# An attention and feed-forward kernel: the load of the next keys asked for by GpSimd behind its seventh subtraction, in place of SyncE ahead of its turns of x rows and forms

## The reference

```python
x = x + xattn(layernorm(x), ctx)       # Q = xn Wq' + bq, K = ctx Wk' + bk
                                       # softmax(Q K' / 32) ctx
x = x + ffn(layernorm(x))              # silu(x Wg') * (x Wu'), then Wd'; weights are
                                       # 4-bit codes, one factor for each block of 64
```

## Time and profile before

| | |
|---|---|
| median of three runs | 1919.1 us |
| the profiled execution | 1918.35 us, its span 1916.2 us |
| granted TensorE clock, mean | 0.999 of full speed |
| busy: PE, DVE, ACT, POOL | 1898.2, 1623.0, 1448.2, 370.3 us |
| GpSimd's subtractions (line 1583) | 64, 893 ns mean |
| transfers of `ctx` by SyncE, 1024 KB each | 8, of which 7 at line 1534 |

### The profile page before, as it was taken

The page is one execution under the profiler, slowest core; times in us unless marked ns, Lnnn a source line. Parts: engine busy times, 40 slices in busy tenths (PEclk is TensorE's granted clock), DMA queues, the critical chain, the costliest instruction groups (busy, mean ns, idle before and its releaser), DMA issues.

```text
span 1916.2 us, 29499 instructions
## 1 busy us (share of the span) xinstructions
PE 1898.2 (99%) x9758; PEld 963.7 (50%) x9758; DVE 1623.0 (85%) x2694; ACT 1448.2 (76%) x2697; POOL 370.3 (19%) x568
## 2 busy tenths in 40 slices
PE   9999999999999999999999999999999999999999
PEld 4487888744444444444444444444444444444444
DVE  7978999869889899899898888898798898896963
ACT  3887776588998988988988988988999999900000
POOL 2023353301111121121121121121123222210110
PEclk9999999999999999999999999999999999999999
DMA  9338999955554565454454454465679988974462
GB/s 356 71 85 189 259 262 276 309 156 130 118 145 125 119 152 130 114 153 130 113 153 126 112 157 120 114 159 134 143 192 225 249 228 217 229 254 131 156 234 84
DMA packets 437640, 326.14 MB, mean 170 GB/s; under 512 B 371680, under 2 KB 371952, under 8 KB 435568
## 3 DMA queue, kind: packets, MB, share of 16 engines
q1 hardware_dynamic: 393280, 170.55, 39.6%
q0 software_dynamic: 44032, 153.65, 25.0%
q10 hardware_dynamic: 176, 0.07, 0.0%
HBM read 154.31 MB, written 82.31 MB: 123 GB/s over the span
## 4 chain that ended last, share of the span: by engine, by line
PE 72%; ACT 12%; DVE 8%; issue 4%; DMA 0%; SPq 0%; DVEq 0%; POOL 0%; ACTq 0%
PE ps L2294 39%; PE ps L2337 23%; PE ps L1682 7%; ACT sq L347 4%; ACT sq L343 3%; PE ps L1650 2%; PE ps L1717 2%; DVE w L363 1%; DVE tail L2447 1%; ACT halves L415 1%; ACT tail L2368 1%; ACT w L347 1%; ACT w L343 1%; ACT tail L2383 1%; DVE halves L431 1%
## 5 line engine op out<-in xcount | busy, mean ns | idle before, releaser
L2294 PE MATMUL ps<-T,wS 128*128 128x512 f16 x4704 | 1017.7, 379 | 5.1 <-DVE ps L2402 2.5
L2294 PEld LDWEIGHTS ps<-T,wS 128*128 128x128 f16 x4704 | 459.6, 98 | 560.0 <-issue 6.7
L347 ACT ACTIVATE sq<-sq 128x512 f32<-128x512 f32 x898 | 516.9, 628 | 0.0
L363 DVE SCALAR_TENSOR_TENSOR w<-sq,w 128x512 f32<-128x512 f32 x590 | 415.9, 705 | 117.0 <-ACT sq L347 107.7
L343 ACT ACTIVATE sq<-q 128x512 f32<-128x512 int32 x598 | 363.9, 632 | 49.1 <-DVE w L363 48.6
L2337 PE MATMUL ps<-T,tail 128*128 128x512 f16 x1584 | 346.7, 380 | 3.9 <-DVE tail L2489 2.7
L2337 PEld LDWEIGHTS ps<-T,tail 128*128 128x128 f16 x1584 | 155.2, 98 | 192.8 <-issue 5.8
L431 DVE SCALAR_TENSOR_TENSOR halves<-w,halves 128x512 f16<-128x512 f32 x240 | 163.0, 688 | 6.4 <-ACT halves L415 6.1
L2337 PE MATMUL ps<-T,wS 128*128 128x512 f16 x768 | 168.4, 379 | 0.0
L2242 POOL DMA_DIRECT2D keep_h<-tail x196 | 106.2, 542 | 292.0 <-DVE tail L2447 291.7
L415 ACT CAST halves<-w 128x512 f16<-128x512 f32 x204 | 126.7, 622 | 43.2 <-DVE w L363 31.6
(11 more groups left out here) (244 smaller groups left out, 1868.6 us busy)
## 6 DMA issues: line engine op xcount, KB each, us to landing
keep_h<-tail POOLq DMA_DIRECT2D x196, 256.0 KB, 2.5
tail<-keep_h POOLq DMA_DIRECT2D x66, 512.0 KB, 4.9
wS<-keep_h POOLq DMA_DIRECT2D x32, 512.0 KB, 4.9
q<-in_L_ffn_down_q POOLq DMA_DIRECT2D x56, 256.0 KB, 4.2
T<-in_x SPq DMA_DIRECT2D x13, 1024.0 KB, 8.6
q<-in_L_ffn_up_q POOLq DMA_DIRECT2D x52, 256.0 KB, 3.0
q<-in_L_ffn_gate_q POOLq DMA_DIRECT2D x48, 256.0 KB, 3.5
keep_x<-T SPq DMA_DIRECT2D x38, 256.0 KB, 4.2
```

The costliest lines, as they stand in the source:

```text
L347: nc.scalar.activation(place, place, ACT.Square, bias=b, scale=a).then_inc(un.s_act, 1)
L363: nc.vector.scalar_tensor_tensor(out=out, in0=square_place(un, u, i - 1), scalar=FACTORS[i - 1][1], in1=un.w[:, buf, :], op0=ALU.add, op1= ...
L2294: last = nc.tensor.matmul(ps[:, bank, :], un.wS[:, z % SLOTS, a, kt, :], t.Tp[side][product][:, :, b, kt, :], start=fresh and n == 0, stop ...
```

## The change

The load of the next keys leaves SyncE's list, where it stood behind the turns of the keys and ahead of the row turns and everything else of the step. It enters GpSimd's list behind the subtraction of group o = 6, ahead of the x form sum that follows that subtraction from step 2 on. The wait on `s_klo` goes with it. The buffer, the size, the semaphore and the count of loads stay.

```diff
     ATT = TB * HALVES
     LAST_ATT_BANKS = (6, 7, 3, 6)
+    CONTEXT_AT = 6
     KEYS_HI_AT = (2, 3)
...
             turn_keys(b, 0)
             turn_keys(b, 1)
-            if b < LAST:
-
-                sp.wait_ge(s_klo, TB * (b + 1))
-                sp.dma_start(keys[:, :, :], t.ctx_t[b + 1]).then_inc(s_keys, 16)
             if b + 1 in BY_DMA:
                 turn_rows(b + 1)
...
                 nc.gpsimd.tensor_tensor(RT[:, 1, o, :], R32[:, o % R_RING, :], RT[:, 0, o, :], ALU.subtract).then_inc(s_rlo, 1)
+                if b < LAST and o == CONTEXT_AT:
+                    pool.wait_ge(s_klo, TB * (b + 1))
+                    nc.gpsimd.dma_start(keys[:, :, :], t.ctx_t[b + 1]).then_inc(s_keys, 16)
                 if b >= 2 and o >= 5:
                     t_sum(pool, nc.gpsimd.tensor_tensor, t, b - 2, o - 5)
```

## The result

The changed kernel takes 1937.34 us, the median of six runs (1935.88 to 1942.73), against 1918.58 us for the kernel before on the same chip (six runs, 1917.31 to 1922.13). The ratio is 1.0098, with an interval of 1.0086 to 1.0111: slower by 18.8 us, outside the forecast's range and above every rival. The profiled execution took 1940.43 us, 3.1 us over its median, with a span of 1938.3 us. It is compared with the profiled execution of before (span 1916.2), so the difference to be found is 22.1 us.

A forecast was written before the change was run, and what follows sets the result against it. TensorE was taken to bound the kernel. Nothing from SyncE's saved issues in steps 2 to 6 and +3.4 us from steps 0 and 1, on a median of 1919.1, gave 1922.5 us (+0.18%), range 1919.3 to 1926.3.

The forecast's parts named there:

- What bounds the kernel: Behind attention TensorE alone sets the time, so a gap put into it during attention moves the end by its length.
- Steps 0 and 1: Attention's first two steps: the later key load is not hidden and TensorE begins step 2 3.4 us late.
- the five large gaps: TensorE waits in step 1 before lines 1636 and 1629, in the attended groups (line 1650), and before line 1682.
- The landing: Time from GpSimd's issue of the key load to its arrival: 5.6 us taken in step 0, bounds 5.1 to 7.3.
- D: VectorE's delay at the key maximum of step 0, waiting for the later load: 5.1 us (4.6 to 6.8).
- the row turns: SyncE's four x row turns in step 1: without the load ahead they speed up, recovering part of the delay.
- upper bound, 6.2 us: Largest lateness of TensorE at the start of step 2, with the longest landing and only 0.6 us won back.
- Rival 2: VectorE's key maximum in step 1 waits again after 7.3 us landings; +6.2 us, 1925.3 to 1927 us; chance 0.20.
- Steps 2 to 6: Later attention steps: the key load is hidden, 3.8 us to spare in step 2, and nothing is gained or lost.
- I cost it at nothing: GpSimd's issue delays its eighth subtraction by at most 0.86 us, hidden before the scores; priced at zero.
- None from step 2 on: The profile after would show no new VectorE key waits or TensorE gaps from step 2 on.
- Rival 3: GpSimd's load descriptors wait for VectorE on their shared port, up to 1.21 us each; at most +4.6 us; chance 0.06.

The follow-up runs named there:

- e1: Kernel before, with GpSimd asking for the next keys in steps 0 and 1 only and SyncE in the others; 1924.72 us, ratio 1.0036.
- e2: Kernel before, with GpSimd asking behind its seventh subtraction in steps 2 to 6 only, SyncE in steps 0 and 1; 1933.13 us, ratio 1.0079.
- e3: Kernel before, all key loads still on SyncE but waiting there for GpSimd's seventh subtraction; 1927.72 us, ratio 1.0052.
- e8: Kernel before, loads on SyncE; in steps 2 to 6 GpSimd waits behind its seventh subtraction for the eighth eviction; 1919.16 us, ratio 1.0002.
- e4: Kernel before, with GpSimd asking behind its last x form sum in steps 2 to 6, SyncE in steps 0 and 1; 1948.73 us, ratio 1.0164.
- e5: Kernel before, with GpSimd asking behind its eighth subtraction in steps 2 to 6; 1932.43 us, ratio 1.0066.
- e6: Kernel before, with GpSimd asking behind its fifth subtraction in steps 2 to 6; 1931.09 us, ratio 1.0061.

## Why the prediction was wrong, point by point

**What bounds the kernel: right.** TensorE's 1539 us behind attention are unchanged, and its gaps in attention add up to the loss.

**Steps 0 and 1: right in mechanism, too small.** The places of the five large gaps were right. The second exponent ended at 135.34 us, forecast 135.3, but that agreement is luck: the prologue ended 0.7 us earlier in this execution, and counted from the start of R the exponent was 5.9 us later than before, not 5.1. The sum was 3.4 us; it is 6.0 in the profile (4.9 of it in named gaps), and e1 has +6.7 us by its medians. Two terms were mis-sized. The landing: 6.4 us in step 0, where 5.6 was taken, which made D 5.8 instead of 5.1. And the row turns: I let them recover part of the delay, but with the load on the other queue they are as slow as ever (9.68 us against 9.12), and the gap before line 1682 grew from 1.3 to 2.50 us. The forecast's own upper bound, 6.2 us, would have held this part. Rival 2's amount, +6.2 and more, was right for this part, but not its mechanism: the second maximum came late (4.10 us of wait, at a landing of 8.0) and its exponents were still in time, since no wait at line 1629 followed in step 2; the turns decided.

**Steps 2 to 6: wrong, and this is the larger part.** The step that failed reads: GpSimd pays 0.86 us, the eighth subtraction comes at most that much later, "I cost it at nothing". The issue did cost GpSimd only 0.74 us and the subtraction was in time (in step 0 it was 1.02 us, and TensorE waited 0.25). What was left out is VectorE: the load changes how the two engines share, and the one VectorE instruction that falls beside GpSimd's next four takes 4.9 to 5.1 us instead of 1.2 to 1.8. With the turned keys, which landed late beside the load (3.4 us of the waits, against 8.3 behind VectorE's late evictions), that makes 2 to 4 us on TensorE in each of five steps, 13.5 us in the profile (11.7 of it in these two waits) and +15.1 us in e2. I costed the edit by who waits for GpSimd, and did not ask who runs beside it. "None from step 2 on" was right for the load (VectorE never waited for it there) and wrong for TensorE.

**Rival 3** had the right pair of engines and the wrong direction. It took the rule of "SBUF — State Buffer" in the Trainium skill, section SBUF: two separate sides, that GpSimd can't write descriptors while VectorE holds the port, and gave at most +4.6 us in all, 1.2 of them from later loads. The runs show GpSimd keeping VectorE out behind its load, and no run here shows the page's direction.

**The trace of before had a sign of it.** In step 7 GpSimd issues a load at 353.20 us, and its subtraction and two sums follow without a pause until 357.55. Beside it, on VectorE of the kernel before:

```profile
355.09 3.01 DVE L363 SCALAR_TENSOR_TENSOR w<-sq,w 128x512 f32<-128x512 f32 x1
```

Its ordinary form lasts 0.68 to 1.78 us. That row is the only one of its kind in attention; the changed kernel has one of 4.07 us at this place (line 1349, at 372.19 us). I used the GpSimd side of the same stretch for the issue's price and did not read VectorE's beside it.

**The turns.** The rule that the Trainium skill gives in "DMA: Bandwidth & Descriptors", section Queues, rings and completion order, is that a DMA engine takes packets from its queues in turn. That the turns would then pass the load, with a sum of 2.6 us, was my working and not the page's: in turn also means that the load takes its share. The measured 9.68 and 10.31 us for four turns, against 9.12 behind a load on their own queue, and landings of 6.4 to 8.0 us for the three turns issued beside the load, against 3.4 for the one ahead of it, speak against the working: even the middle course that I took was too hopeful.

**What is settled and what is not.** Shown: the loss of steps 2 to 6 needs GpSimd's load (e3 and e8 have none, and no loss there) and does not need those of steps 0 and 1 (e2). The long VectorE instruction goes with the GpSimd work that is ready behind the load (e4: none behind it, no long instruction; e5: two sums, 2.3 to 2.7 us in four of five steps), and in e5 an instruction that reads PSUM escaped it. Open: why the load has this effect, and why VectorE got in twice in e6. No run shows whether a forced pause behind the load or a load of a few bytes would avoid it; that it is GpSimd's load as such, whatever its size, is not shown.

## What to carry to other kernels

An instruction put into one engine's list is to be priced on the engines that run beside it, too: read what the engines run in the stretch behind it, side by side, before calling the issue free. Keep GpSimd's loads away from a place where several GpSimd instructions stand ready behind them while VectorE combines two SBUF tensors on the path; a load from SyncE at the very same moment cost nothing in steps 2 to 6. Look also at what the old place kept apart: SyncE's turns and the load shared one queue in a fixed order, and on two queues the turns issued beside the load landed late. Where a transfer changes its issuing engine, take its landing time from that engine's loads under the same traffic, and do not credit the queue that it left with a speedup.

## What the hardware showed that was not expected

- *GpSimd's load and VectorE.* Without a load GpSimd and VectorE take turns, which costs GpSimd 0.44 us an instruction. Behind a load in steps 2 to 6 of the changed kernel, GpSimd's four ready instructions run at full speed (1.25 and 0.67 us), and a VectorE instruction with both inputs in SBUF ends half a microsecond after the last of them. With seven ready (e6) VectorE got in twice; with one input in PSUM it was not held (0.69 us, e5).
- *Landing.* The same 1 MB to the same buffer at the same point took 5.2 us from SyncE and 6.4 from GpSimd (step 0); in company GpSimd's took 7.5 to 9.6 us (steps 1 to 6 of the changed kernel), and up to 12.4 when asked for at the end of the step (e4).
- *Turns beside a load.* The last of SyncE's four key turns, issued within a microsecond of GpSimd's load, landed after 8.0, 9.5 and 9.0 us in steps 4 to 6 of the changed kernel. In the kernel before, with the load behind the turns on one queue, the slowest turn of those steps took 3.4, 3.4 and 5.7 us.
- *The clock.* Behind gaps of 4.2 to 6.4 us (e3, e4) TensorE's granted clock was 0.50 to 0.64 over the next 24 matmuls, which cost another 1.4 to 2.5 us; behind the gaps of up to 2.5 us in the changed kernel the same 24 matmuls took 2.79 us, at full clock. The gaps of 4.2 to 6.4 us therefore cost 6.7 to 8.9.
